# Layer-0 router: logits made token by expert, an earlier low half, experts merged by a mask product, four down banks

## The reference, cut to what matters

```python
x = x + ga * L0_attn(h)                       # h = layernorm(x) * (1 + ca) + sa
h = layernorm(x) * (1 + cb) + sb
logits = h @ gate_weight.T                    # 4096 x 8
probs = softmax(logits); top_w, top_i = top_k(probs, 2)
top_w = top_w / clip(sum(top_w), 1e-12)
primary_mask[top_i[:, 0]] = True              # experts that are first for any token
sim = where(primary_mask[None, :], similarity_matrix, -inf)
best_j, best_sim = argmax(sim, -1), max(sim, -1)
expert_map = where(~primary_mask & (best_sim >= 0.7), best_j, arange(8))
combine = weights added up at expert_map[top_i]
y = einsum(silu(g) * u, down_proj)            # g, u = h @ gate_up_proj, for all 8 experts
x = x + gb * einsum('ne,enh->nh', combine, y)
```

## Time and profile before

| | us |
|---|---|
| median of 3 runs | 914.73 (913.86 to 918.37) |
| the profiled execution | 918.26 |
| its span in the trace | 916.4 |

### The profile page before, as it was taken

The page is one execution under the profiler, slowest core; times in us unless marked ns, Lnnn a source line. Parts: engine busy times, 40 slices in busy tenths (PEclk is TensorE's granted clock), DMA queues, the critical chain, the costliest instruction groups (busy, mean ns, idle before and its releaser), DMA issues.

```text
span 916.4 us, 22613 instructions
## 1 busy us (share of the span) xinstructions
PE 803.8 (88%) x8710; PEld 553.1 (60%) x8710; DVE 576.4 (63%) x1587; ACT 387.7 (42%) x765; POOL 271.2 (30%) x268
## 2 busy tenths in 40 slices
PE   4765989999989989999999999988999799999940
PEld 3452556666645646656656566555567688889940
DVE  8476776666689988677687786876556222222218
ACT  3583221222256315625346254465654343444423
POOL 2580000000176510012020120214776244544430
PEclk9796999999979959999999999999999799999985
DMA  6700131427205952134241342222324167777746
GB/s 199 297 1 1 36 138 34 167 93 245 80 1 151 316 152 59 29 101 93 50 106 27 101 96 49 60 41 59 79 72 140 51 187 209 212 216 218 229 125 212
DMA packets 107827, 108.37 MB, mean 118 GB/s; under 512 B 48892, under 2 KB 93644, under 8 KB 106796
## 3 DMA queue, kind: packets, MB, share of 16 engines
q1 hardware_dynamic: 103196, 97.82, 37.1%
q0 software_dynamic: 4544, 9.35, 2.9%
HBM read 82.15 MB, written 44.78 MB: 139 GB/s over the span
## 4 chain that ended last, share of the span: by engine, by line
PE 57%; DVE 19%; DMA 7%; issue 6%; ACT 5%; POOL 4%; SPq 2%; POOLq 0%; DVEq 0%; ACTq 0%
PE bank L1975 7%; PE bank L2204 6%; PE bank L2214 5%; PE bank L1801 5%; PE bank L1812 5%; PE bank L1813 5%; DVE sb_arena L1400 5%; PE bank L1867 4%; PE bank L1915 4%; DMA expert_results<-sb_arena 4%; PE bank L1893 2%; PE bank L2123 2%; PE bank L1842 2%; PE bank L2133 2%; DVE sb_ST L1089 1%
## 5 line engine op out<-in xcount | busy, mean ns | idle before, releaser
L1400 DVE TRANSPOSE_TENSOR_REDUCE sb_arena<-bank 128x16 f32<-128x512 f32 x192 | 120.3, 685 | 24.9 <-PE bank L1915 23.6
L967 ACT ACTIVATE sb_arena<-bank 128x512 f32<-128x512 f32 x192 | 99.2, 602 | 41.1 <-PE bank L1915 41.1
L1055 ACT ACTIVATE sb_arena<-bank,sb_arena 128x256 f32<-128x256 f32 x156 | 65.3, 471 | 99.0 <-PE bank L2204 98.3
L791 POOL DMA_INDIRECT expert_results<-sb_arena x78 | 74.7, 957 | 93.5 <-DVE sb_arena L1668 81.0
L891 ACT ACTIVATE sb_arena<-bank 128x512 f32<-128x512 f32 x64 | 38.1, 597 | 143.5 <-PE bank L1813 143.5
L1801 PEld LDWEIGHTS bank<-sb_arena 128*128 128x128 f32 x512 | 68.2, 196 | 41.9 <-issue 25.7
L2204 PE MATMUL bank<-sb_arena 128*128 128x256 f32 x312 | 79.1, 398 | 5.0 <-DVE sb_arena L1664 4.8
L1801 PE MATMUL bank<-sb_arena 128*128 128x128 f32 x512 | 70.5, 281 | 10.0 <-DVE sb_arena L1227 10.0
L2214 PE MATMUL bank<-sb_arena 128*128 128x128 f32 x624 | 76.2, 276 | 0.0
L1227 DVE TENSOR_TENSOR sb_arena<-sb_arena,bank 128x512 f32<-128x512 f32 x64 | 43.6, 684 | 49.7 <-ACT sb_arena L891 49.5
L2214 PEld LDWEIGHTS bank<-sb_arena 128*128 128x128 f32 x624 | 73.2, 193 | 0.1
(11 more groups left out here) (265 smaller groups left out, 1371.3 us busy)
## 6 DMA issues: line engine op xcount, KB each, us to landing
sb_arena<-in_w SPq DMA_DIRECT2D x39, 578.0 KB, 4.1
dispatched_rows<-in_padding SPq DMA_DIRECT2D x8, 2064.0 KB, 9.6
sb_arena<-dispatched_rows SPq DMA_DIRECT2D x39, 129.0 KB, 2.2
sb_arena<-q_parts SPq DMA_DIRECT2D x8, 512.0 KB, 5.7
sb_arena<-k_parts SPq DMA_DIRECT2D x8, 512.0 KB, 7.0
context_rel<-sb_arena SPq DMA_DIRECT2D x256, 8.0 KB
sb_arena<-expert_results SPq DMA_DIRECT2D x16, 256.0 KB, 6.1
q_parts<-sb_arena SPq DMA_DIRECT2D x24, 128.0 KB, 3.3
```

The costliest lines, as they stand in the source:

```text
L791: nc.gpsimd.indirect_dma_start(yD[:, :], bass.IndirectOffsetOnAxis(ap=rid[:, k, r:r + 1], axis=0), YS[:, k, r, :], None).then_inc(s_yo[k], 16)
L967: nc.scalar.activation(dst, src, ACT.Exp).then_inc(s_ex, 1)
L1400: v.tensor_reduce(dst.rearrange("p h b -> p (h b)"), bank[r % RING][:, :].rearrange("p (b c) -> p b c", c=32), AX, ALU.max, apply_transpos ...
```

## The change

- `logits0(c)` now makes one chunk: four matmuls with 128 tokens of `hT` as weights and 8 gate columns streaming, straight into token by expert order (bank 2 for the low, bank 6 for the high half). `logits_out`, `logits_back` and the tile `LT` are gone.
- VectorE normalises chunks 4 and 7 (`normalise2nd`), ScalarE the others.
- ScalarE's exponential of the low half stands behind `features0(1, 5)`, ahead of the features of chunks 6 and 7.
- `second` needs one instruction less. Hidden products 0 and 1 stand ahead of `second(high)`.
- Per token weights by original expert (`EQ`) are made before the counts arrive. The map becomes an 8 x 8 mask `smq`; `WD` is made by multiplying `EQ` with it and adding over experts (`merged`): experts 0 and 1 first, 2 to 4 and 5 to 7 within the first round, after accumulations 7 and 10.
- Hidden products 2 and 3 are made before the weights of the round are copied and before the first accumulation.
- `down0` uses banks 4 to 7 and waits for accumulation u-4.

```diff
+        BY_VECTOR = (4, 7)
+        def gate_bank(h):
+            return bank[6 if h else 2]
...
-                normalise1st(1, c)
+                if c not in BY_VECTOR:
+                    normalise1st(1, c)
                 if c:
                     features0(1, c - 1)
-                if c == 5:
-                    logits_out(0)
+                if c == 6:
+                    act.wait_ge(s_lgh, 1)
+                    nc.scalar.activation(PR[:, 0:NT // 2, :], LG[:, 0:NT // 2, :], ACT.Exp).then_inc(s_elh, 1)
             features0(1, NC - 1)
-            logits_out(1)
-            act.wait_ge(s_lgh, 1)
-            nc.scalar.activation(PR[:, 0:NT // 2, :], LG[:, 0:NT // 2, :], ACT.Exp).then_inc(s_elh, 1)
...
+            def normalise2nd(c):
+                wait(dve, s_tr, NC + c - 1)
+                for t in range(TPC):
+                    T = c * TPC + t
+                    if t == TPC - 1:
+                        dve.wait_ge(s_xn, NC + c)
+                    ins = v.tensor_scalar(XN[:, c % 2, t, :], X[:, T, :], MV[:, T, 0:1], RSTD[:, T:T + 1],
+                                          ALU.subtract, ALU.mult)
+                ins.then_inc(s_xn, 1)
...
-                link(v.tensor_tensor(CD[:, ts, :], PR[:, ts, :], OH1[:, ts, :], ALU.subtract))
-                link(v.scalar_tensor_tensor(out=CD[:, ts, :], in0=OH1[:, ts, :], scalar=-4.0, in1=CD[:, ts, :],
+                link(v.scalar_tensor_tensor(out=CD[:, ts, :], in0=OH1[:, ts, :], scalar=-5.0, in1=PR[:, ts, :],
...
+            link(v.tensor_tensor(smq[:, :, :], emap[:, :].unsqueeze(1).to_broadcast([P, E, E]),
+                                 apart[:, :, :].rearrange("p i j -> p j i"), ALU.is_equal))
+            def merged(lo, n):
+                shape = [P, n, NT, E]
+                part = parts[:, 0:n * NE].rearrange("p (n t e) -> p n t e", n=n, t=NT)
+                link(v.tensor_tensor(part, EQ[:, :, :].unsqueeze(1).to_broadcast(shape),
+                                     smq[:, lo:lo + n, :].unsqueeze(2).to_broadcast(shape), ALU.mult))
+                link(v.tensor_reduce(WD[:, lo:lo + n, :], part, AX, ALU.add))
+            merged(0, 2)
+            hidden0(2, 2)
+            hidden0(3, 3)
...
-                    if not first or j >= 2:
+                    if not first or j >= 4:
                         hidden0(u, j)
                     if j:
-                        accumulate(0, u - 1, j - 1, bank[4 + (j - 1) % 2])
+                        accumulate(0, u - 1, j - 1, bank[4 + (j - 1) % 4])
+                        if first and j in (8, 11):
+                            merged(2 if j == 8 else 5, 3)
...
+            def logits0(c):
+                pe.wait_ge(s_hT, NC + c + 1)
+                for t in range(TPC):
+                    T = c * TPC + t
+                    at = T % (NT // 2) * E
+                    ins = mm(gate_bank(c // 4)[:, at:at + E], hT[:, T * P:(T + 1) * P], gateT[:, 0:E], start=True, stop=True,
                              skip_group_check=True)
+                if c % 4 == 3:
+                    ins.then_inc(s_cnt, 1)
...
-                wait(pe, s_acc[0], u - 1)
+                wait(pe, s_acc[0], u - 3)
```

More of the change, by code:

```diff
@@ L166, in build @@
         bs, bj, cnd, emap = [table(E) for _ in range(4)]
-        LT = R.take(2 * CH).rearrange("p (s n) -> p s n", s=2)
+        parts = R.take(3 * NE)
+        apart = R.take(E * E).rearrange("p (i j) -> p i j", i=E)
+        R.take(2 * CH - 3 * NE - E * E)
         id1, id2 = [R.take(NT) for _ in range(2)]
@@ L863, in _ @@
             steps0(1)
-            def logits_out(g):
-                act.wait_ge(s_lt, 2 * g + 1)
-                nc.scalar.copy(LT[:, g, :], bank[2 + g][:, :]).then_inc(s_lt, 1)
             deviation(1, 0)
@@ L1230, in _ @@
             low, high, every = slice(0, NT // 2), slice(NT // 2, NT), slice(0, NT)
+            iotaj = iota[:, :].unsqueeze(1).to_broadcast([P, E, E])
+            link(v.tensor_tensor(apart[:, :, :], iotaj, iota[:, :].unsqueeze(2).to_broadcast([P, E, E]), ALU.subtract))
             dve.wait_ge(s_cnt, 1)
@@ L1254, in _ @@
[L1254 to L1257 removed]
+            link(v.tensor_scalar(pm[:, :], bank[7][:, 16:16 + E], 0.5, None, ALU.is_lt))
+            unused = pm[:, :].unsqueeze(1).to_broadcast([P, E, E])
+            link(v.scalar_tensor_tensor(out=sm[:, :, :], in0=unused, scalar=LOWEST, in1=sim[:, :, :],
+                                        op0=ALU.mult, op1=ALU.add))
@@ L1258, in _ @@
             link(v.tensor_reduce(bs[:, :], sm[:, :, :], AX, ALU.max))
             link(v.tensor_tensor(smc[:, :, :], sm[:, :, :], bs[:, :].unsqueeze(2).to_broadcast([P, E, E]), ALU.is_lt))
-            iotaj = iota[:, :].unsqueeze(1).to_broadcast([P, E, E])
-            link(v.scalar_tensor_tensor(out=smc[:, :, :], in0=smc[:, :, :], scalar=float(E), in1=iotaj,
+            v.scalar_tensor_tensor(out=cnd[:, :], in0=bs[:, :], scalar=THRESHOLD, in1=pm[:, :], op0=ALU.is_ge, op1=ALU.mult)
+            link(v.scalar_tensor_tensor(out=smc[:, :, :], in0=smc[:, :, :], scalar=float(E), in1=apart[:, :, :],
@@ L1754, in outputs @@
                 ins.then_inc(s_y, 1)
-            def logits0(g):
-                pe.wait_ge(s_hT, NC + 4 * g + 4)
-                for j in range(4):
-                    ins = mm(bank[2 + g][32 * j:32 * j + 32, :], gateT[:, :], chunk(hT, 4 * g + j), start=True, stop=True,
-                             skip_group_check=True)
-                ins.then_inc(s_lt, 1)
-            def logits_back(g):
-                pe.wait_ge(s_lt, 2 * g + 2)
-                for t in range(TPC):
-                    ins = nc.tensor.transpose(bank[6 + g][:, t * P:(t + 1) * P], LT[:, g, t * P:(t + 1) * P], ident[:, :])
-                ins.then_inc(s_cnt, 1)
+            def logits0(c):
[4 more added lines that the diff above has]
+                    ins = mm(gate_bank(c // 4)[:, at:at + E], hT[:, T * P:(T + 1) * P], gateT[:, 0:E], start=True, stop=True,
+                             skip_group_check=True)
+                if c % 4 == 3:
+                    ins.then_inc(s_cnt, 1)
             for c in range(2, 6):
@@ L1779, in _ @@
                     transposes0(1, c - 4)
-            transposes0(1, 4)
             pe.wait_ge(s_wm[0], 16 * 3)
             logits0(0)
+            transposes0(1, 4)
+            logits0(1)
+            logits0(2)
             transposes0(1, 5)
+            logits0(3)
+            transposes0(1, 6)
             pe.wait_ge(s_gt, NC)
-            logits_back(0)
-            transposes0(1, 6)
+            logits0(4)
             transposes0(1, 7)
-            logits0(1)
-            logits_back(1)
+            for c in range(5, NC):
+                logits0(c)
             def counts():
```

46 lines of the change are left out of this document (14 added, 32 removed).

## The result

| | before | after |
|---|---|---|
| median of 20 runs, measured side by side | 916.93 (911.84 to 921.47) | 910.63 (908.24 to 917.37) |
| the profiled execution | 918.26 | 910.99 |
| its span | 916.4 | 909.2 |

The ratio is 0.9941, with a 95% interval of 0.9927 to 0.9954: 6.3 us (by the medians) off the kernel before, where 6.0 were forecast. The forecast of 908.7 was made from a median of before of 914.73; in the joint measurement that median was 2.2 higher. So the difference came out as forecast to 0.3, and the time itself 1.9 above the 908.7.

What follows compares the result with a forecast made beforehand. TensorE bounds the first expert loop, so the question was when hidden product 2 starts: 2.9 + 0.65 + 3.45 = 7.0 earlier, less 1.0 for the clock, gives 6.0, so 914.73 - 6.0 = 908.7; range 904 to 912.5.

Steps and rivals of the forecast that it cites:

- Transposes of chunk 6 at 66.75: TensorE before the logits: chunk 6's transposes start at 66.75 instead of 66.99, after waiting for ScalarE's normalisation.
- 40 passes at 0.214: TensorE from chunk 6's transposes: 40 transpose and logits passes in a row take 8.6 us, logits complete about 75.5.
- Rival B: Clock stays at 2.4 GHz through the logits: ready at 72.6, another 2.9 earlier, 905 with the gap's loss; chance 0.15.
- The clock through the logits: TensorE's granted clock stays at the low level, 1.2 GHz, during the narrow logits passes, giving 75.5 rather than 72.6.
- High shift 2.9 earlier: VectorE's shift of the high half of the logits starts at 75.6 in place of 78.47, 2.9 us earlier.
- The 3.3 us taken off ScalarE are worth 0.2: Moving normalisation of chunks 4 and 7 to VectorE gains only 0.2, since ScalarE then waits for VectorE's scales.
- What is won is that the low half's work no longer stands behind: Before the high shift: the gain comes from the low half's VectorE work no longer standing behind the logits copies and transposes.
- "second" 0.65 and the block behind the counts 3.45: VectorE after the high shift: one instruction fewer per half saves 0.65; the merge block takes 4.6 instead of 8.07, saving 3.45.
- The clock in the gap, 0 or 1.7: TensorE's wait of about 3 us before down product 2: a clock fall would cost 1.7; 1.0 was put for it.
- Rival C: More given back: merge reading 1.4, loop stalls up to 2.2, late second activation 1.1; 911 to 913; chance 0.27.
- D: Slower than before: logits passes do not overlap weight loads; all lost from 0.44 us a pass, about 923 at 0.7; chance 0.03.
- E: ScalarE waits for VectorE at the early exponential, over 3 us beyond its table load for a loss; some 912, counted in Rival C.

Runs made afterwards that it cites:

- filled logits: Changed kernel plus six added matmuls of 128x256, results unused, in TensorE's waits between transposes and logits of chunks 4 to 7; ratio 0.9905 to the kernel before.
- late exponential: Changed kernel with the low half's exponential back behind the features of chunk 7; ratio 0.9947 to the kernel before.
- wide logits: Changed kernel with router logits expert by token again, with ScalarE's copies and the transposes back, exponential still early; ratio 0.9914 to the kernel before.
- old merge: Changed kernel with the old map, 256-element instructions and WD in one go behind the counts; ratio 0.9971 to the kernel before.
- fill the gap: Changed kernel plus four added matmuls of 128x512, results unused, in TensorE's wait before down product 2; ratio 0.9941 to the kernel before.
- two banks: Changed kernel with two down banks again, down0 waiting for accumulation u-2; ratio 0.9982 to the kernel before.
- filled kernels: Changed kernel plus six unused 128x256 matmuls between the logits, alone (ratio 0.9905) or with four of 128x512 before down product 2 (0.9881).
- fill all: Changed kernel plus unused matmuls between the logits, before down product 2 and, two of 128x512, at the first round's end; ratio 0.9905 to the kernel before.

## Why the prediction held, step by step

**The sum held; one step in it failed.** It had 7.0 us at hidden product 2 and 5.3 or 7.0 in the steady loop, by whether the clock falls in the gap. Measured were 6.68, and with the fall 5.20. The medians differ by 6.3. The 1.1 between this and the profiled 5.2 was not traced to a place; the single profile has one fall in the gap and none at the round's end, the medians mix all combinations. That the medians meet the forecast of 6.0 to 0.3 is therefore in part luck: the place that the sum was made for moved by 5.20, after a shift 0.5 better than forecast, a wait for the second activation 0.5 worse and a clock term 0.5 too small.

- **Transposes of chunk 6 at 66.75.** Measured 65.99, with a prelude 0.5 earlier: right to 0.25.
- **40 passes at 0.214.** 17.05 - 8.45 = 8.60 us, 8.6 forecast; the granted clock was 0.51. Rival B did not happen by itself. Built by hand it gave 2.55 at down product 2, where the rival said 2.9.
- **The clock through the logits.** The trace agrees with the low level: 0.51 from 62.5 to 80. By the Trainium skill (TensorE: Matmul & The Clock Gate, Part 4: PE-mode transpose) transposes do not count as activity for the clock the way matmuls do; that speaks for 12 of the 52 passes from 63.36 on, and of the 8-column matmuls it says nothing. The rows say that these did not hold the clock either: with filled logits it fell in the midst of sixteen of them.
- **High shift 2.9 earlier.** 3.38 measured: 0.26 is chunk 6's start, the rest rounding in the forecast's chain (66.75 + 8.6 was carried as 75.5, and 75.6 for the shift).
- **"The 3.3 us taken off ScalarE are worth 0.2": the step that failed.** ScalarE did wait for VectorE's scales as forecast, and VectorE normalised chunk 4 in 1.10 (chunk 7 took 2.24, while GpSimd was setting memory beside it, but was done 1.5 ahead of its transposes). The step compared chunk 6 with that of the kernel before, and let its transposes wait for ScalarE alone. But between the transposes of chunks 4 and 6 the changed kernel has 24 logits passes that the old one did not have, 5.1 us at the low clock, and without VectorE's share TensorE is the one that is late, in a row from chunk 4 to the shift. Undoing this edit alone cost 1.85 at the shift and 1.4 at down product 2. It is worth that much in the changed kernel since chunk 4's transposes come 1.2 earlier and 16 of the passes still run at 2.4 GHz.
- **"What is won is that the low half's work no longer stands behind": half right.** It is 1.8 of the 3.4, and has two edits for it of which either does; the other 1.5 are the normalisation. The text gave that role to both edits at once and none to the third.
- **"second" 0.65 and the block behind the counts 3.45.** The block from 85.20 to 89.86 takes 4.66 (4.6 forecast, 8.07 before: 3.41 saved), the two instructions on 512 elements 0.69 each, exactly on the straight line; no price for the four-dimensional reading. Undone, the merge cost 2.1 and the rest of the saving is the reordering of hidden products 2 and 3, as forecast. From the shift to L1264 it was 10.61 against 10.50 before, in which 0.65 less work and 0.67 of waiting for the second activation cancel. That wait was put at 0.2 with 1.1 as its bound; it is 0.67 after and 0 in seven other profiles. The clock came back at 22.5 from the last scan output after, and at 19.6 to 20.2 in the four of the seven whose shift stands within 0.25 of after's (late exponential, wide logits, old merge, fill the gap), which is the likely reason.
- **Four banks.** Needed, as said: two cost 1.96.
- **Merges in the loop at nothing.** The two down products behind them took 1.12 and not 1.05, and what follows each starts 0.07 later: 0.14 together.
- **The clock in the gap, 0 or 1.7.** It fell in every profile of a changed kernel without added matmuls there, and cost 1.4 to 1.7 in five (down product 2 to 4: 6.70 to 7.02, against 5.32 where it did not fall), 2.1 with two banks (7.45) and 2.9 to 3.0 in three (8.24, 8.25 and 8.34). So 1.0, an even bet between falling and not, was too little.

Rival C did not come about: of its three mishaps the reading cost nothing, the loop 0.14 and the second activation 0.67. D's passes at 0.44 or more were nowhere, and E's wait did not occur: the exponential follows its table load at once (68.16).

**Sums among the rivals.** Three do not follow from the forecast's own terms. B with the gap's loss is 914.73 - 7.0 - 2.9 + 1.7 = 906.5, not 905. C's two mishaps and the clock's 1.7 leave 1.7 to 2.8 of the 7.0, not 2 to 4. D at 0.3 a pass ends the logits at 78.5, where nothing is left of the 2.9 and about 4.1 is won, not 4.5. None of them touches the 6.0.

**What stays open.** Why the same added matmuls held the clock in two profiles and not in the third, and why the clock falls in some gaps of 2.3 to 2.4 and not in others, no run here separates. Whether the filled kernels are faster than the changed one in the median is likely (0.988 and 0.9905 against 0.9941) but not shown, as the intervals meet.

## What to carry to other kernels

An edit that replaces a few wide matmuls by many narrow ones changes which engine is late: count TensorE's passes between all the points it used to wait at, at the lower clock, before pricing what another engine gives up. When two edits remove the same obstacle, undo them singly and together; singly each looked worthless here (0.1 and 0.24), together they were worth 1.8. And look at what stands behind a new gap of TensorE, not only at its length: here gaps of 3.5 to 6.1 us cost 1.4 to 3.0 more in slow matmuls behind them.

## What the runs showed of the hardware

- **Eight-column float32 passes with 128-column weights take 0.11 to 0.12 us at a granted clock of 1.00 and 0.21 at 0.50** (16 in 1.85, 24 in 5.13). At half the clock they take twice as long. From 62.5 to 80.0 after, TensorE was busy 16.63 of 17.50 us with them, transposes and the first up matmuls, and the granted clock was 0.51: it came back only at 80.0, during the 512-column up matmuls. In fill all it came back at 68.5, during narrow passes, 1.5 behind two added matmuls of 256 columns.
- **One fall of the clock has no fixed price.** Behind the same gap it was 1.4 to 1.7 in five kernels and 2.9 to 3.0 in three. The three dear ones had the clock low for about twice as long: it was back 3.1 us behind the start of down product 2 after (36.1 from the last scan output), and 6.0 behind it with the normalisation on ScalarE (40.5). In the logits, a fall 7 us later (12.8 from the last scan output, not 5.4), with six added matmuls, brought the shift from 17.05 to 14.78.
- **ScalarE's table load of 1.28 is issued before the exponential's data are there**, as the forecast had assumed. After, VectorE's last shift of the low half ends at 67.75, the load runs from 66.86, and the exponential at 68.16 adds only 0.31:

```profile
67.46 0.29 DVE L1223 TENSOR_TENSOR sb_arena<-bank,sb_arena 128x128 f32<-128x128 f32 x1
66.86 1.28 ACT L881 ACT_TABLE_LOAD   x1
68.16 0.31 ACT L881 ACTIVATE sb_arena<-sb_arena 128x128 f32<-128x128 f32 x1
```
